# Fewer DMA transfers per sequence, constant rows loaded per home, late expert weights split on ScalarE and GpSimd, and new order lists for every engine

## The chip, the cores and the metric

The kernel runs on 1 core of a Trainium2 chip. The metric is device time in microseconds. Five engines work side by side, each through its own list of instructions in order: TensorE (PE, matrix products), VectorE (DVE), ScalarE (ACT), GpSimd (POOL), and SyncE (SP), which here issues every DMA transfer. They meet at semaphores only.

## The reference

One transformer layer on x of 16 sequences, 512 tokens, 128 features: layer norm, causal attention of 16 heads of size 64, a residual with a second layer norm (gamma, beta), layer norm again, and a mixture of 32 experts (top 8) with all experts computed for all tokens.

```python
q = jnp.einsum('bsd,hde->bhse', x, Wq); k = ...; v = ...
scores = jnp.where(causal, q k^T / sqrt(64), -inf); attn = softmax(scores)
y = x + heads @ Wo;  y = layernorm(y, eps=1e-3) * gamma + beta;  x = x0 + y
probs = softmax(h @ gate_w.T); top_w, top_idx = top_k(probs, 8); comb = normalised weights
for each expert: acc += (u * silu(g)) @ dw.T * w_e        # g, u = split(h @ guw.T)
```

## The kernel before

**Numbers.** Every float32 operand is used as a pair of float16 tiles, high and low, and a product is three matmuls (high*high, high*low, low*high). So for each product ScalarE writes the high half out of PSUM and VectorE the low half (`qk_high`/`qk_low`, `v_high`/`v_low`, `h_high`/`h_low`, `o_high`/`o_low`). For the softmax numerators ScalarE makes `p32` and `p_hi`, GpSimd `p_lo` (`p_low`, L1497).

**Order.** The order on each engine is written out by hand as a list of calls, `scores(n, 2, 1); values(n, 4, V); ...`. The second argument group names the PSUM bank (G, U, V, R0, R1; S0 and S1 belong to the scores, XB to the experts' sum). Sequences 0 and 1 are a prologue, a loop `for n in range(2, B - 2)` of 12 passes holds the steady state (each pass mixes the attention of sequence n with the experts of n - 2 and n - 1 and the projections of n + 1), and sequences 14 and 15 an epilogue, all with lists of their own.

**One head's scores.** Keys and queries of a pair of heads (`project`) are put by SP into one of five homes of `score_ops` (`place_qk`, L307 to L312, six transfers). Row maxima go around a longer way: `max_scores` (PE), `row_maximum` (DVE, L1124), `split_maxima` (POOL, L1486 to L1490), `turn_maxima` (PE), `copy_maxima` (ACT, L786), `place_max` (SP, L321, four transfers), and only then may `scores(m, 4g, 0)` start. Besides these, each home holds constant rows (the causal bars). Before the loop GpSimd copies them from the last home into the nine other halves (L1531, four copies of 64x4608 float16), on `rows_filled`.

**Experts.** `gate_product`, `gate_tanh`, `gate_times_tanh`, `up_product`, `times_up` (L1224) make a unit of two experts. The routing weights go to DRAM (`keep_weights`, L327, four transfers) and come back spread over 64 partitions for each of the two experts (`spread_weights`, L335, two transfers a unit). GpSimd multiplies (`weigh_unit`, L1512) and makes the low half (`unit_low`, L1516), PE does `down_product`. For the last sequence VectorE multiplies in float32 (`weigh_last`) and no halves are made.

**Weights.** They are loaded as float32 and split once, in 11 parts of `SPLIT`: w_hi by ScalarE (`halve`, L790), w_lo by VectorE (`rest`, L1067). Parts 0 and 1 (Wq, Wk) are on the way to the first projection, 2 and 3 are Wv and Wo, 4 to 10 the experts'. Their scales come from `largest`, `diagonal` (L1052) and `powers` on VectorE. A sequence has 103 transfers: 48 of `place_qk`, 16 of `place_max`, 4 of `keep_weights`, 32 of `spread_weights`, and 3 of x and y.

Of the kernel before, what the change touches and what calls it, by code (L numbers as in the profile page):

```python
# [11 lines left out]
P = 128  # L12
# [3 lines left out]
C = S // P  # L16
# [19 lines left out]
PARTS = 11  # L36
# [17 lines left out]
def layer(nc, x, wq, wk, wv, wo, gamma, beta, gate, gate_up, down, ident_c, mask_c,  # L54
          key_rows_c, query_rows_c, tail_c, out):
    with ExitStack() as ctx:
# [219 lines left out]
        def _(sp):  # L276
# [25 lines left out]
            def place_qk(m, q):  # L302
                slot = slot_of(m, q)
                if m == 0 and q == 2:
                    sp.wait_ge(w_lo_done, 3)
# [8 lines left out]
            def place_max(m, g):  # L314
                wait(sp, score_mm, UNITS * 2 * (m * PAIRS + 2 * g + 1 - SLOTS + 1))
                sp.wait_ge(rowmaxT_ready, m * QUADS + g + 1)
# [12 lines left out]
            def spread_weights(p, j):  # L329
                if j == 0:  # L330
                    sp.wait_ge(comb_stored, 16 * C * (p + 1))
# [14 lines left out]
            sp.wait_ge(w_lo_done, 2)  # L346
            place_qk(0, 0); load_xb(0); load_x(1); place_qk(0, 1); place_max(0, 0); place_qk(0, 2); place_qk(0, 3)
            place_qk(0, 4); place_max(0, 1); place_qk(0, 5); load_x(2); place_qk(0, 6); place_max(0, 2); place_qk(0, 7)
            place_max(0, 3); place_qk(1, 0); place_qk(1, 1); place_qk(1, 2); place_max(1, 0); place_qk(1, 3)
            place_qk(1, 4); place_max(1, 1); load_xb(1); place_qk(1, 5); place_max(1, 2); place_qk(1, 6)  # L350
            keep_weights(0); spread_weights(0, 0); spread_weights(0, 1); load_x(3); place_qk(1, 7); spread_weights(0, 2)
            spread_weights(0, 3); place_max(1, 3); spread_weights(0, 4); spread_weights(0, 5); spread_weights(0, 6)
            place_qk(2, 0); place_qk(2, 1); spread_weights(0, 7); spread_weights(0, 8); spread_weights(0, 9)
            place_max(2, 0); place_qk(2, 2); spread_weights(0, 10); place_qk(2, 3); spread_weights(0, 11)
            spread_weights(0, 12); spread_weights(0, 13); spread_weights(0, 14); place_qk(2, 4)

            for n in range(2, B - 2):
                place_max(n, 1); spread_weights(n - 2, 15); load_x(n + 2); place_qk(n, 5); place_max(n, 2)
                place_qk(n, 6); store(n - 2); place_qk(n, 7); keep_weights(n - 1); spread_weights(n - 1, 0)
                spread_weights(n - 1, 1); spread_weights(n - 1, 2); spread_weights(n - 1, 3); place_max(n, 3)  # L360
                spread_weights(n - 1, 4); place_qk(n + 1, 0); spread_weights(n - 1, 5); spread_weights(n - 1, 6)
                spread_weights(n - 1, 7); load_xb(n); place_qk(n + 1, 1); spread_weights(n - 1, 8)
                spread_weights(n - 1, 9); place_qk(n + 1, 2); place_max(n + 1, 0); spread_weights(n - 1, 10)
                spread_weights(n - 1, 11); place_qk(n + 1, 3); spread_weights(n - 1, 12); spread_weights(n - 1, 13)
                spread_weights(n - 1, 14); place_qk(n + 1, 4)

            place_max(14, 1); spread_weights(12, 15); place_qk(14, 5); place_qk(14, 6); place_max(14, 2); load_xb(14)
            store(12); place_qk(14, 7); keep_weights(13); spread_weights(13, 0); spread_weights(13, 1)
            spread_weights(13, 2); spread_weights(13, 3); spread_weights(13, 4); place_max(14, 3); spread_weights(13, 5)
            place_qk(15, 0); spread_weights(13, 6); spread_weights(13, 7); place_qk(15, 1); spread_weights(13, 8)  # L370
            place_max(15, 0); spread_weights(13, 9); spread_weights(13, 10); place_qk(15, 2); place_qk(15, 3)
            spread_weights(13, 11); spread_weights(13, 12); place_max(15, 1); place_qk(15, 4); spread_weights(13, 13)
            spread_weights(13, 14); spread_weights(13, 15); place_qk(15, 5); place_max(15, 2); place_qk(15, 6)
            load_xb(15); place_qk(15, 7); store(13); keep_weights(14); spread_weights(14, 0); spread_weights(14, 1)
# [3 lines left out]
            spread_weights(14, 14); spread_weights(14, 15); store(14); load_down(15); keep_weights(15)  # L378
# [8 lines left out]
        def _(pe):  # L387
# [73 lines left out]
            def scores(m, h, u):  # L461
# [1170 lines left out]
```

## Time and profile before

| | |
|---|---|
| median of 3 runs | 1748.65 us (1747.98 to 2051.43) |
| the profiled execution, its own time | 1747.59 us |
| its span, first to last instruction | 1745.7 us |
| mean granted TensorE clock | 0.991 |
| PE busy | 1633.9 us, 94% |
| DVE, ACT, POOL busy | 1462.4, 1404.4, 1403.9 us (84%, 80%, 80%) |

The page of the profile gives busy time by engine. Its list of waits says which engine stood idle for whom. The windows view splits the span into stretches, and the timeline lists instructions in order of time with the idle time before each in square brackets. PE's waits appear twice, for the matmul (PE) and for its weight load (PEld).

### The profile page before, as it was taken

What the parts mean: (1) busy time and instruction counts of PE and PEld (TensorE: products, weight loads), DVE (VectorE), ACT (ScalarE), POOL (GpSimd) and SP (SyncE); (2) the same over time, 40 slices, a digit from 0 to 9 for tenths busy, and PEclk for the clock granted to TensorE, in tenths of its full rate; (3) what the DMA queues carried; (4) which work ended last, traced back from release to release, by engine and by line L of the source; (5) the groups of instructions that cost most, each with busy time, mean ns of one, the idle gap of its engine ahead of it and who ended that gap; (6) DMA issues with size and microseconds to landing.
All of it is one profiled execution on the core that took longest, in us unless ns stands there. A gap on an engine that the chain in (4) does not pass through costs nothing.

```text
span 1745.7 us, 56980 instructions
## 1 busy us (share of the span) xinstructions
PE 1633.9 (94%) x21209; PEld 1113.7 (64%) x21209; DVE 1462.4 (84%) x4484; ACT 1404.4 (80%) x2364; POOL 1403.9 (80%) x1164
## 2 busy tenths in 40 slices
PE   3799999999999999999999999999999999999868
PEld 1366766666666666666666666666676666667655
DVE  7999889797887978879797887979889797887757
ACT  2799888797887879788797888879788787888752
POOL 4477997888879788887888979788897888889880
PEclk9999999999999999999999999999999999999999
DMA  5554554646455464544646454473645546435423
GB/s 181 128 122 106 145 136 123 166 106 158 104 132 129 106 178 110 142 115 115 174 106 159 110 140 124 104 186 95 158 117 133 139 106 165 123 109 138 112 79 105
DMA packets 219444, 226.26 MB, mean 130 GB/s; under 512 B 27041, under 2 KB 185249, under 8 KB 218913
## 3 DMA queue, kind: packets, MB, share of 16 engines
q1 hardware_dynamic: 219168, 222.61, 49.8%
q8 instruction: 170, 2.79, 0.7%
q14 instruction: 106, 0.86, 0.2%
HBM read 82.53 MB, written 5.24 MB: 50 GB/s over the span
## 4 chain that ended last, share of the span: by engine, by line
PE 61%; SPq 8%; DVE 8%; DMA 6%; POOL 6%; issue 5%; ACT 5%; POOLq 0%; ACTq 0%; DVEq 0%
PE bank_r L389 15%; PE bank_s L389 12%; PE bank_v L389 8%; PE bank_g L389 8%; PE bank_u L389 8%; PE bank_x L389 7%; SPq L321 3%; POOL p_lo L1497 2%; DMA expert_room<-comb_rows 2%; SPq L335 2%; SPq L311 1%; SPq L312 1%; POOL expert_room L1512 1%; DMA xt<-in_x 1%; SPq L310 1%
## 5 line engine op out<-in xcount | busy, mean ns | idle before, releaser
L1497 POOL TENSOR_TENSOR p_lo<-p,p_hi 128x1280 f16<-128x1280 f32 x256 | 674.7, 2636 | 149.0 <-ACT p_hi L786 148.2
L848 ACT ACTIVATE p<-bank_s,back 128x512 f32<-128x512 f32 (+1 forms) x768 | 461.4, 615 | 61.9 <-PE bank_s L389 53.8
L389 PE MATMUL bank_s<-score_ops 128*128 128x62 f16 (+10 forms) x4096 | 405.6, 233 | 20.6 <-DMA score_ops<-rowmaxT 15.3
L389 PEld LDWEIGHTS bank_s<-score_ops 128*128 128x128 f16 x4096 | 278.1, 97 | 192.5 <-issue 46.8
L1512 POOL TENSOR_TENSOR expert_room<-expert_room 128x512 f32<-128x512 f32 x240 | 304.4, 1275 | 34.7 <-DMA expert_room<-comb_rows 17.4
L786 ACT ACTIVATE p_hi<-p 128x1280 f16<-128x1280 f32 x256 | 324.6, 1268 | 7.8 <-PE bank_r L389 2.2
L1516 POOL TENSOR_TENSOR halves<-expert_room,halves 128x512 f16<-128x512 f32 x240 | 276.4, 1162 | 29.0 <-ACT halves L786 27.3
L1124 DVE CUSTOM_DVE_ANT_0 max_junk<-bank_r,mask 128x384 f16<-128x384 f32 (+3 forms) x523 | 232.1, 474 | 36.6 <-PE bank_g L389 16.3
L389 PE MATMUL bank_x<-w_hi,halves 128*128 128x128 f16 x1920 | 199.1, 220 | 2.0 <-POOL halves L1516 2.0
L786 ACT ACTIVATE halves<-expert_room 128x512 f16<-128x512 f32 x240 | 150.1, 625 | 44.8 <-POOL expert_room L1512 32.2
L389 PE MATMUL bank_x<-w_lo,halves 128*128 128x128 f16 x960 | 173.2, 220 | 0.0
L389 PEld LDWEIGHTS bank_x<-w_hi,halves 128*128 128x128 f16 x1920 | 155.2, 98 | 20.3 <-issue 6.2
L389 PE MATMUL bank_r<-nat 64*128 64x384 f16 (+3 forms) x523 | 106.1, 300 | 15.3 <-DVE o L1137 9.8
L1124 DVE CUSTOM_DVE_ANT_0 max_junk<-bank_u,mask 128x512 f16<-128x512 f32 (+3 forms) x202 | 99.0, 505 | 6.1 <-PE bank_g L389 4.0
L389 PE MATMUL bank_r<-tanh_room,w_hi 128*128 128x512 f16 x338 | 101.8, 383 | 0.5 <-DVE o L1137 0.4
L389 PEld LDWEIGHTS bank_x<-w_lo,halves 128*128 128x128 f16 x960 | 94.1, 98 | 7.3
L389 PE MATMUL bank_r<-v_hi,p_hi 128*128 128x65 f16 x870 | 87.9, 194 | 2.1 <-POOL p_lo L1497 1.4
L389 PE MATMUL bank_r<-v_hi,p_lo 128*128 128x65 f16 x870 | 87.9, 194 | 0.0
L389 PE MATMUL bank_r<-v_lo,p_hi 128*128 128x64 f16 x870 | 87.8, 192 | 0.0
L786 ACT ACTIVATE nat<-bank_r 128x512 f16<-128x512 f32 x110 | 65.9, 599 | 26.2 <-PE bank_r L389 24.1
L389 PE MATMUL bank_u<-tanh_room,w_hi 128*128 128x512 f16 x264 | 78.7, 380 | 7.5 <-DVE v_lo L1112 6.2
L1124 DVE DVE_READ_ACCUMULATOR2_ANT rowmax<- 128x1 f32 x1024 | 85.2, 83 | 0.1
(298 smaller groups left out, 5015.4 us busy)
## 6 DMA issues: line engine op xcount, KB each, us to landing
score_ops<-nat SPq DMA_DIRECT2D x256, 256.0 KB, 3.8
score_ops<-nat SPq DMA_DIRECT2D x512, 128.0 KB, 3.6
expert_room<-comb_rows SPq DMA_DIRECT2D x480, 128.0 KB, 3.0
xt<-in_x SPq DMA_DIRECT2D x16, 256.0 KB, 3.5
xb<-in_x SPq DMA_DIRECT2D x16, 256.0 KB, 4.1
score_ops<-rowmaxT SPq DMA_DIRECT2D x256, 2.0 KB
out_y<-expert_room SPq DMA_DIRECT2D x16, 256.0 KB, 3.4
score_ops<-comb_rows SPq DMA_DIRECT2D x32, 128.0 KB, 3.0
```

Source lines behind the costliest of these rows:

```text
L310: sp.dma_start(score_ops[0:E, 0:4, slot, ab, :], home[rows, K_HI:K_HI + 1].to_broadcast([E, 4, S])).then_inc(placed[q], 16)
L311: sp.dma_start(score_ops[0:E, 4:6, slot, ab, :], home[rows, Q_HI:Q_LO + 1]).then_inc(placed[q], 16)
L312: sp.dma_start(score_ops[E:P, 0:5:4, slot, ab, :], home[rows, K_LO:Q_HI + 1]).then_inc(placed[q], 16)
L321: sp.dma_start(home[part:part + 1], rowmaxT[at:at + 8, :]).then_inc(max_placed[g], 16)
L335: sp.dma_start(weighed(p, j)[ED * e:ED * e + ED, :], comb_rows[2 * j + e:2 * j + e + 1, :].to_broadcast([ED, S])).then_inc(spread_sem(p, j ...
L389: return pe.matmul(dst, lhsT, rhs, start=start, stop=stop, skip_group_check=shared)
L786: return act.activation(dst, src, ACT.Copy)
L848: act.activation(p32[:, h % P_SLOTS, at:at + cols], bank[score_bank(h, u)][:, 0:cols], ACT.Exp, scale=back[:, SC_SCORE:SC_SCORE + 1]).then ...
L1124: done = dve.tensor_tensor_reduce(max_junk[:, k % 2, at:at + cols], bank[b][:, at:at + cols], mask[:, S - cols:S], 1.0, NEG, ALU.add, ALU. ...
L1497: pool.tensor_tensor(p_lo[:, slot, :], p32[:, slot, :], p_hi[:, slot, :], ALU.subtract).then_inc(p_lo_done, 1)
L1512: pool.tensor_tensor(weighed(p, j), weighed(p, j), unit(p, j), ALU.mult).then_inc(a32_done, 1)
L1516: pool.tensor_tensor(a_lo[:, j % 2, :], weighed(p, j), a_hi[:, j % 2, :], ALU.subtract).then_inc(a_lo_done, 1)
```

## The change

1. Transfers. `place_max` issues 2 and not 4 (both rows at once), `keep_weights` 1 and not 4, `spread_weights` 1 and not 2 for a unit (128 partitions). A sequence has 76 and not 103. What waits for them counts 32, 16 and 16 instead of 64, 64 and 32.
2. Constant rows. The one load into the last home and GpSimd's four copies are gone. `fill_rows(slot)` loads both halves of a home from DRAM by two transfers (384 KB and 128 KB), ten in all, put between the first placings. `place_max` of sequence 0 waits on SP for them.
3. Late weights. Parts 4 to 10: ScalarE makes w_hi as before and then scales the source in place, GpSimd subtracts (`rest_late`). VectorE keeps parts 0 to 3.
4. `weigh_last` moves from VectorE to GpSimd.
5. All five lists are written anew. Nothing is computed differently, and each list holds the same calls apart from those named above.

```diff
+            def fill_rows(slot):
+                sp.dma_start(score_ops[E:P, 1:4, slot], key_rows_c).then_inc(rows_filled[slot], 16)
+                sp.dma_start(QB[E:P, slot], query_rows_c).then_inc(rows_filled[slot], 16)
...
-                    for part in range(2):
-                        at = 16 * k + 8 * part
-                        sp.dma_start(home[part:part + 1], rowmaxT[at:at + 8, :]).then_inc(max_placed[g], 16)
+                    sp.dma_start(home, rowmaxT[16 * k:16 * k + 16, :]).then_inc(max_placed[g], 16)
...
-                for c in range(C):
-                    sp.dma_start(comb_rows[:, c * P:c * P + P], combT[c * NE:c * NE + NE, :]).then_inc(comb_stored, 16)
+                sp.dma_start(comb_rows.rearrange("e (c p) -> c e p", c=C), combT).then_inc(comb_stored, 16)
...
-                for e in range(2):
-                    sp.dma_start(weighed(p, j)[ED * e:ED * e + ED, :],
-                                 comb_rows[2 * j + e:2 * j + e + 1, :].to_broadcast([ED, S])).then_inc(spread_sem(p, j), 16)
+                both = comb_rows[2 * j:2 * j + 2].rearrange("a (b s) -> a b s", b=1)
+                sp.dma_start(weighed(p, j), both.to_broadcast([2, ED, S])).then_inc(spread_sem(p, j), 16)
...
+                if part >= EARLY:
+                    w = SPLIT[part][0]
+                    act.activation(source(part), source(part), ACT.Copy, scale=w_scale[:, w:w + 1]).then_inc(late_scaled, 1)
...
+            def rest_late(part):
+                w, at, cols = SPLIT[part]
+                pool.wait_ge(w_hi_done, part + 1)
+                pool.wait_ge(late_scaled, part - EARLY + 1)
+                pool.tensor_tensor(wl(w, at, cols), source(part), wh(w, at, cols), ALU.subtract).then_inc(late_lo_done, 1)
...
-            pool.wait_ge(ln_shift[0], 1)
-            pool.wait_ge(rows_loaded, 80)
-            for side in (KB0, KB1, KB2, QB):
-                rows = side[E:P].rearrange("p a b s -> p (a b) s")
-                pool.tensor_copy(rows[:, 0:2 * SLOTS - 1, :], rows[:, 2 * SLOTS - 1:2 * SLOTS, :].to_broadcast([E, 2 * SLOTS - 1, S])).then_inc(rows_filled, 1)
...
-                spread_weights(n - 1, 9); place_qk(n + 1, 2); place_max(n + 1, 0); spread_weights(n - 1, 10)
+                place_max(n + 1, 0); spread_weights(n - 1, 10); place_qk(n + 1, 2); spread_weights(n - 1, 11)
```

**SP, in the loop, around `place_max(n + 1, 0)`.** Rows of before: the spreading of two units, `place_qk(n + 1, 2)`, then the four transfers of `place_max`, then two more units.

```order
L335 DMA expert_room<-comb_rows 64x512 x4
L310 DMA score_ops<-nat 64x4x512
L311 DMA score_ops<-nat 64x2x512
L312 DMA score_ops<-nat 64x2x512
L310 DMA score_ops<-nat 64x4x512
L311 DMA score_ops<-nat 64x2x512
L312 DMA score_ops<-nat 64x2x512
L321 DMA score_ops<-rowmaxT 1x8x128 x4
L335 DMA expert_room<-comb_rows 64x512 x4
```

The same place of the change:

```order
L339 DMA expert_room<-comb_rows 128x1x512 x3
L326 DMA score_ops<-rowmaxT 2x8x128 x2
L339 DMA expert_room<-comb_rows 128x1x512
L314 DMA score_ops<-nat 64x4x512
L315 DMA score_ops<-nat 64x2x512
L316 DMA score_ops<-nat 64x2x512
```

`place_max(n + 1, 0)` now stands ahead of `place_qk(n + 1, 2)` and is two transfers long.

**GpSimd, in the prologue, behind the first norm.** Rows of before, from the last instruction of `inverse_deviation` to `keep_h(0)`:

```order
L1472 TENSOR_TENSOR shift<-minus_mean,rstd 128x4
L1531 COPY score_ops<-score_ops 64x4608 x4
L1486 TENSOR_SCALAR rowmax<-rowmax 128x16
L1488 CAST turnable<-rowmax 128x2x8
L1490 TENSOR_TENSOR turnable<-rowmax,turnable 128x2x8
L1480 COPY h_cur<-h 128x512
```

The same place of the change:

```order
L1472 TENSOR_TENSOR shift<-minus_mean,rstd 128x4
L1486 TENSOR_SCALAR rowmax<-rowmax 128x16
L1488 CAST turnable<-rowmax 128x2x8
L1490 TENSOR_TENSOR turnable<-rowmax,turnable 128x2x8
L1496 TENSOR_TENSOR w_lo<-expert_room,w_hi 128x1024 x2
L1480 COPY h_cur<-h 128x512
```

The four copies are gone from the head of the list, and the first two of seven `rest_late` (L1496) stand behind `split_maxima(0, 0)`; the others follow one by one among the `p_low` of sequence 0.

## Rows read from the trace of the kernel before

**Rows 1.** Windows view, from the span's start; first row names the columns.
```profile
core 0: us, PE busy (x) PEld busy (x) DVE busy (x) ACT busy (x) POOL busy (x), PEclk, DMA share, GB/s
24.00:58.00 34.00, 20.92 (x75) 6.46 (x76) 31.66 (x70) 11.29 (x19) 8.35 (x6) 0.95 0.33 78
58.00:131.00 73.00, 65.02 (x928) 44.28 (x927) 67.81 (x232) 66.56 (x107) 47.88 (x32) 0.98 0.59 136
...
234.50:1485.50 1251.00, 1209.31 (x15950) 829.79 (x15949) 1062.55 (x3324) 1051.86 (x1777) 1064.18 (x889) 1.00 0.52 132
1485.50:1692.00 206.50, 194.79 (x2592) 134.55 (x2590) 156.27 (x463) 162.95 (x272) 179.80 (x145) 0.99 0.42 111
1692.00:1745.70 53.70, 39.37 (x247) 25.64 (x243) 37.65 (x80) 15.22 (x27) 2.74 (x6) 0.87 0.35 110
```

**Rows 2.** Waits in 234:1486, PE then PEld: total us, times, longest.
```profile
PE bank_s L389 <- DMA score_ops<-rowmaxT: 14.9, 12, 2.2
PE bank_r L389 <- DVE o L1137: 9.8, 12, 0.9
PE bank_u L389 <- DVE v_lo L1112: 6.2, 5, 1.4
PE bank_x L535 <- DVE comb L1210: 4.4, 12, 0.4
...
PEld bank_r L389 <- DVE hT L1102: 10.9, 12, 1.0
```

**Rows 3.** Timeline of the prologue: start, duration, engine, instruction, idle before.
```profile
13.24 17.93 POOL L1531 COPY score_ops<-score_ops 64x4608 f16<-64x4608 f16 x4 [6.26 <-DMA tail<-in_tail]
13.40 9.90 DVE L1067 SCALAR_TENSOR_TENSOR w_lo<-score_ops,w_scale,w_hi 128x1024 f16<-128x1024 f32 x2 [1.22 <-ACT w_hi L790]
...
23.96 1.03 PE L389 MATMUL bank_r<-hT,w_hi 128*128 128x512 f16 x2 [11.93 <-DVE hT L1102]
...
27.27 3.92 DVE L1052 TENSOR_SCALAR w_diagonal<-ident,w_peak 2x2 f32<-2x2 f32 x1
```

**Rows 4.** Single lines of the kernel: duration in ns, min/median/max.
```profile
L1067 DVE SCALAR_TENSOR_TENSOR w_lo<-expert_room,w_scale,w_hi x4: 1254/1278/2015, 76.4 to 98.4; 128x1024 f16<-128x1024 f32 x4
...
L1052 DVE TENSOR_SCALAR w_diagonal<-ident,w_peak x3: 218/219/3921, 10.1 to 56.4; 11x11 f32<-11x11 f32 x1, 2x2 f32<-2x2 f32 x1, 7x7 f32<-7x7 f32 x1
...
L790 ACT ACTIVATE w_hi<-expert_room,w_scale x4: 1132/1139/1148, 59.2 to 81.3; 128x1024 f16<-128x1024 f32 x4
...
L1497 POOL TENSOR_TENSOR p_lo<-p,p_hi x256: 2607/2623/3653, 68.5 to 1675.8; 128x1280 f16<-128x1280 f32 x128
```

**Rows 5.** Timeline 520 to 534: ACT, SP and PE around `place_max(n + 1, 0)`.
```profile
525.73 0.27 ACT L786 ACTIVATE rowmaxT<-bank_v 32x128 f16<-32x128 f32 x1 [1.39 <-PE bank_v L389]
...
524.12 0.74 SPq L310 DMA_DIRECT2D score_ops<-nat  x1
...
528.96 2.80 SPq L321 DMA_DIRECT2D score_ops<-rowmaxT  x4
...
532.93 0.38 PE L389 MATMUL bank_s<-score_ops 128*128 128x512 f16 x1 [0.75 <-DMA score_ops<-rowmaxT]
```

**Rows 6.** Timeline 76 to 99, a low half on VectorE beside GpSimd.
```profile
77.18 6.48 POOL L1497 TENSOR_TENSOR p_lo<-p,p_hi 128x1280 f16<-128x1280 f32 x2 [2.14 <-ACT p_hi L786]
79.16 2.02 DVE L1067 SCALAR_TENSOR_TENSOR w_lo<-expert_room,w_scale,w_hi 128x1024 f16<-128x1024 f32 x1
```

**Rows 7.** DMA issues: count, KB each, median us to landing (page, part 6).
```profile
expert_room<-comb_rows SPq DMA_DIRECT2D x480, 128.0 KB, 3.0
```

**Rows 8.** The last stage: timeline, chain of waits, and GpSimd's weighing (ns).
```profile
1715.90 20.45 SPq L335 DMA_DIRECT2D score_ops<-comb_rows  x32
...
1738.58 3.58 PE bank_x L389 x32
...
L1512 POOL TENSOR_TENSOR expert_room<-expert_room x16: 1263/1279/1310, 1018.4 to 1089.5; 128x512 f32<-128x512 f32 x16
```

More of the change, by code:

```diff
@@ L315, in place_max @@
                 wait(sp, score_mm, UNITS * 2 * (m * PAIRS + 2 * g + 1 - SLOTS + 1))
+                if m == 0:
+                    for slot in range(2 * g, min(2 * g + 2, SLOTS)):
+                        sp.wait_ge(rows_filled[slot], 32)
                 sp.wait_ge(rowmaxT_ready, m * QUADS + g + 1)
@@ L351, in _ @@
[L351 to L355, printed above, removed]
@@ new lines, in _ @@
+            scores(1, 2, 1); max_scores(1, 4, 0, G, U); project(1, 10, R1); times_wo(0, 3, V); scores(1, 2, 2)
+            values(1, 5, G); turn_maxima(1, 1, U); scores(1, 3, 0); scores(1, 3, 1); max_scores(1, 4, 1, R0, V)
+            times_v(1, 0, U); scores(1, 3, 2); project(1, 11, R1); times_v(1, 1, V); max_scores(1, 4, 2, G, R0)
+            scores(1, 4, 0); max_scores(1, 5, 0, R1, U); project(1, 12, G); values(1, 6, R0); scores(1, 4, 1)
+            times_v(1, 2, V); scores(1, 4, 2); project(1, 13, U); scores(1, 5, 0); times_v(1, 3, R1)
@@ new lines, in _ @@
+            turn_heads(1, 0, G); scores(1, 5, 1); max_scores(1, 5, 1, V, R0); scores(1, 5, 2); values(1, 7, R1)
+            project(1, 14, U); turn_h2(0); max_scores(1, 5, 2, R0, G); turn_heads(1, 1, V); scores(1, 6, 0)
+            times_v(1, 4, R1); gate_product(0, 0, G); turn_maxima(1, 2, R0); logit_product(0); scores(1, 6, 1)
+            gate_product(0, 1, R1); scores(1, 6, 2); max_scores(1, 6, 0, U, G); times_wo(1, 0, V); scores(1, 7, 0)
+            turn_h(2, R0); project(1, 15, U); scores(1, 7, 1); times_v(1, 5, V); scores(1, 7, 2)
@@ new lines, in _ @@
+            max_scores(1, 7, 2, G, R1); up_product(0, 3, R0); scores(1, 10, 2); turn_heads(1, 3, U); times_v(1, 8, G)
+            scores(1, 11, 0); values(2, 0, R0); project(2, 2, R1); gate_product(0, 5, U); times_wo(1, 1, G)
+            times_v(1, 9, V); up_product(0, 4, R0); turn_maxima(1, 3, R1); down_product(0, 0); max_scores(2, 0, 0, G, U)
+            max_scores(2, 0, 1, R1, R0); project(2, 3, V); scores(1, 11, 1); scores(1, 11, 2); gate_product(0, 6, U)
+            values(2, 1, R1); max_scores(2, 0, 2, R0, G); scores(1, 12, 0); down_product(0, 1); up_product(0, 5, R0)
@@ new lines, in _ @@
+            up_product(0, 8, V); project(2, 5, G); scores(1, 15, 0); scores(1, 15, 1); down_product(0, 4)
+            max_scores(2, 2, 0, U, V); turn_maxima(2, 0, R0); times_wo(1, 2, R1); times_v(1, 13, U)
+            max_scores(2, 2, 1, V, G); scores(1, 15, 2); gate_product(0, 9, R1); down_product(0, 5)
+            gate_product(0, 10, U); turn_heads(1, 6, V); max_scores(2, 2, 2, R1, R0); scores(2, 0, 0); scores(2, 0, 1)
+            project(2, 6, R1); up_product(0, 9, G); down_product(0, 6); project(2, 7, R0); times_v(1, 14, V)
@@ new lines, in _ @@
+            scores(2, 0, 2); times_v(1, 15, R1); max_scores(2, 3, 0, V, G); project(2, 8, U); up_product(0, 10, R0)
+            project(2, 9, V); down_product(0, 7); turn_heads(1, 7, R1); down_product(0, 8); max_scores(2, 3, 1, U, G)
+            gate_product(0, 11, R0); scores(2, 1, 0); scores(2, 1, 1); times_wo(1, 3, R1); max_scores(2, 3, 2, U, R0)
+            scores(2, 1, 2); times_v(2, 0, G); down_product(0, 9); up_product(0, 11, U); scores(2, 2, 0)
+            gate_product(0, 12, V); turn_maxima(2, 1, R1); down_product(0, 10)
@@ new lines, in _ @@
+            max_scores(14, 7, 1, U, V); scores(14, 9, 2); times_wo(14, 0, R1); scores(14, 10, 0); project(15, 0, R0)
+            turn_weights(13); scores(14, 10, 1); scores(14, 10, 2); gate_product(13, 1, U); up_product(13, 0, V)
+            up_product(13, 1, G); times_v(14, 8, R0); times_v(14, 9, V); project(15, 1, R1); turn_heads(14, 3, U)
+            max_scores(14, 7, 2, R0, G); gate_product(13, 2, V); scores(14, 11, 0); up_product(13, 2, R1)
+            gate_product(13, 3, R0); values(15, 0, G); times_wo(14, 1, V); turn_heads(14, 4, R1)
```

1190 lines of the change are left out of this document (584 added, 606 removed).

## The prediction

> **What bounds the kernel.** I read the windows view first. In the steady loop [rows 1] PE is busy for 1209.31 of 1251.00 us, in 12 passes of 104.25 us each. VectorE, ScalarE and GpSimd are each busy for about 85% of it. So PE's own products set the loop, and at most 1251.00 − 1209.31 = 41.7 us are there to be taken. Outside the loop it differs. In the stretch 24 to 58 PE is busy for 20.92 of 34 us and VectorE for 31.66: VectorE sets the pace. In 58 to 131 three engines are all near 90% (65.02, 67.81, 66.56 of 73). The epilogue has 206.50 − 194.79 = 11.7 us idle.
>
> The waits of PE in the loop come next [rows 2]. The maxima's last transfer ends a wait of 14.9 us in 12 times (once a pass), hT of VectorE 10.9 us and o 9.8 us (12 each), v_lo 6.2 us in 5, comb 4.4 us in 12. The timeline of the prologue [rows 3] shows one large wait: PE's first projection starts at 23.96 after 11.93 us of waiting for hT, which VectorE could not make before its two `rest`.
>
> **The change, in the order of time.**
>
> *Constant rows.* GpSimd's four copies run from 13.24 for 17.93 us [rows 3]. Two `rest` of 128x1024 lie beside them and take 9.90 us, where the four late ones have a median of 1.278 [rows 4]. Without copies the two take 2 × 1.28 = 2.6, so 7.3 us go from the path to the first projection. One of the tiny `w_diagonal` beside the copies takes 3.92 and not 0.22 us [rows 3, 4], 3.7 us more, again on VectorE where it is the bound. Together 11.0.
>
> A rule of the Trainium skill bears on this (SBUF — State Buffer, section "Who interferes with whom"): a VectorE instruction with two SBUF inputs contends with a GpSimd instruction that reads SBUF, and whichever starts first holds the shared ports throughout. The 9.90 us fit it in kind. It also speaks against item 3 below, where I come back to it.
>
> What replaces the copies is ten transfers on SP. An issue on SP costs 0.64 to 0.74 us [rows 5, 8], so 6.4 to 7.4 us of SP time, spread between the first placings, when SP's next hard need is the placing of maxima for the first scores. I take 0; the cover is SP's free time before the first placing, and if that is gone it costs the whole 7.4.
>
> *Late weights.* VectorE loses seven `rest`: four of 1024 columns (4 × 1.28 = 5.1) and three smaller ones, some 8 us in all. GpSimd gets seven `rest_late`. Their price isn't in the trace; the nearest row is `p_low`, also a subtraction of an fp16 half, with 2.62 us for 1280 columns [rows 4], so 2.62 × 1024/1280 = 2.1 each, under 15 us, less than the 17.93 it loses. ScalarE gets six or seven in-place scalings at 1.14 [rows 4], some 7 us, and in 58 to 131 it has 73 − 66.6 = 6.4 us free [rows 1]. So VectorE's relief is about eaten up by ScalarE. I take −1; bounds +7 (all of it on ScalarE as bound) and −8 (all of VectorE's relief).
>
> Beside it, from rows: one `rest` beside a `p_low` took 2.02 us in place of 1.28 [rows 6], so a `rest_late` that runs beside VectorE's `rest(3)` costs 0.7 us. By the Trainium skill's rule in that same section the loser stands for the whole of the other's instruction, which by the estimate above would be 2.1 us. That would make the sum 35 or 34 where it is 36 below. The row, a third of an instruction rather than all of it, is the nearer guide, and neither changes the forecast.
>
> Prologue: −11 − 1 = **−12**, bounds −19 and −4 (fills not hidden).
>
> *The loop.* Take the first scores of a pass [rows 5]. `copy_maxima` ends at 525.73 + 0.27 = 526.0. SP is then still in the six placings of `place_qk(n + 1, 2)` that it began at 524.12, and starts the four transfers of the maxima only at 528.96, ending 2.80 us later (0.70 each). PE starts the scores at 532.93, after 0.75 us of waiting. Now SP has `place_max` ahead of `place_qk`, and two transfers: 526.0 + 1.4 = 527.4 for the last issue, in place of 531.76. That is 4.4 us earlier, with a longest wait of 2.2 [rows 2]. So all 14.9 go.
>
> hT's 10.9: two more `qk_high` now stand ahead of `h_high` on ScalarE, but more of PE's work (`scores`, `times_wo`) stands between the turn of h and the next use of bank R1. I take half, 5. v_lo's 6.2: the same, 3. comb's 4.4: the wait is at most 0.4 each, and several PE groups (`values`, two `up_product`) now stand in between; all 4.4. o's 9.8: same neighbours, so 0. Gain 14.9 + 5 + 3 + 4.4 = 27.4.
>
> Against it: at two places, groups 0 and 2, `turn_maxima` now follows the last `max_scores` after less PE work, so VectorE's `row_maximum` and GpSimd's `split_maxima` have less time. Where GpSimd is in a `p_low` just then, 2.62 us are added [rows 4]. No row shows a wait there now. The bounds are 0 and 2 × 2.62 = 5.2 us a pass (63 us in 12); I take 0.5 a pass, 6 us: less PE work stands between than before, but some still does. Loop: **−21**, bounds −40 (all idle time) and, below, the slower rival.
>
> Fewer issues by themselves (27 a sequence) relieve SP only; they count where SP is waited for, which is in the 14.9.
>
> *The end.* `weigh_last` on GpSimd: 16 × 1.279 = 20.5 us [rows 8]. The first spreading is issued at 1715.90 and lands 3.0 us later [rows 7, 8]: GpSimd starts about 1719.5 and ends about 1740.0. Three transfers fewer for `keep_weights` (3 × 0.64 = 1.9) bring this to 1738.1, beside PE's last products at 1738.58 to 1742.16 [rows 8]. So it is just hidden: 0, or up to +2 if `keep_weights` isn't what is waited for. With the spreading halved from 32 to 16 issues, SP (20.45 us before) is no longer what paces it. The epilogue's new order: I take −3 of its 11.7 idle [rows 1], as the same placings wait there; bounds 0 and −8.
>
> **Sum.** −12 − 21 − 3 = −36. The profiled execution's own time is 1747.59, so 1711.6. The median of before lies 1.1 above it, so I forecast **1712 us**. The line at 2%, about what a measurement of this kernel can tell from no change, is 1748.65 × 0.98 = 1713.7. The forecast stands almost on it.
>
> **The rivals.**
>
> *A, nearly all waits go.* For it: PE's idle in the loop is 41.7 us, and each wait is short (0.4 to 2.2 each), so a better order can hide them. Taking 19 in the prologue, 31 in the loop and 8 at the end gives 1748.65 − 58 = 1691. Against it: ends of waits are handed on to the next engine.
>
> *B, the loop's gain is handed on.* VectorE and GpSimd at 85% of the loop have dense parts; a wait removed in front of them comes back behind. Then the loop keeps 2 us, with the prologue's 12 and 3: about 1732. For it: hT, o, v_lo and comb are all VectorE's. Against it: the largest, 14.9, is SP's own order.
>
> *C, slower.* GpSimd holds `split_maxima` behind a `p_low` at both places in each pass. Then 5.2 us a pass in place of 0.5: 1712 + (63 − 6) = 1769. It decides the sign once the new wait is above 0.5 + 36/12 = 3.5 us a pass. Against it: GpSimd idles 15% of the loop, and PE's cover absorbs part.
>
> *D, the change doesn't do what it says in the loop and the prologue waits for SP's fills.* Prologue −4, the rest 0 to −3: about 1743.
>
> **Chances.** Forecast (1700 to 1724) 0.50; A 0.18; B 0.20; C 0.07; D 0.05. The range has to leave out no more than 2 in 10: C, D and the better half of A go out, so 1692 to 1741. Faster by over 2% (below 1713.7): half of the forecast's 0.50 and a little more (0.30), and A: 0.48. Within 2%: the other 0.20, B, D, and those of C's weaker forms: 0.49. Slower by over 2%: 0.03. The forecast case's own range is 1700 to 1724.
>
> **What would show it.** In the profile after: the two early `rest` together near 2.6 us, PE's first projection at about 16.7, no `w_diagonal` above 0.3 us, and first scores some 9 to 11 us earlier. In 58 to 131 ScalarE is not above 97%. In the loop a pass takes about 102.5 us, PE's wait for the maxima's transfer is gone, and the new waits (`turn_maxima` for GpSimd's halves) add up to less than 10 us. At the end PE works without a break through the last units. The forecast is wrong if the first projection still waits for something else (the loads of x or of the weights), if the wait for maxima comes back as one for GpSimd or VectorE, or if PE waits for GpSimd in the last stage.

## The result, and the profile after

The changed kernel takes 2502.96 us (median of 4 runs, 2502.35 to 2505.06), where the kernel before takes 1750.16 beside it. The ratio is 1.431, with a 95% interval of 1.428 to 1.434. So it is 43% slower, where I forecast 1712 us and gave slower 3 in 100. One of the four runs of the kernel before was a slow one (2051.43 us); the ratios here compare fast runs only. No rival came near it: the slowest, C, was 1769.

The profiled execution has a span of 2500.6 us against 1745.7. Windows of the changed kernel, in the columns of [rows 1]: the two prologue stretches, then from PE's first to its last instruction of the loop, and a piece of the last stage.

```profile
24.00:58.00 34.00, 22.82 (x108) 8.40 (x109) 30.57 (x95) 20.02 (x31) 10.49 (x12) 0.85 0.82 173
58.00:131.00 73.00, 69.09 (x1030) 48.23 (x1029) 61.99 (x227) 70.96 (x119) 56.58 (x43) 1.00 0.61 142
253.90:2075.60 1821.70, 1340.22 (x15951) 887.52 (x15949) 1059.77 (x3312) 1045.38 (x1777) 1066.78 (x889) 0.86 0.34 90
2430.00:2470.00 40.00, 25.63 (x94) 15.57 (x94) 6.72 (x10) 2.75 (x4) 10.11 (x8) 0.62 0.13 50
```

To 131 us all is well: PE is busy for 69.09 us of 73 where it was 65.02. Behind it a pass of the loop takes 1821.7 / 12 = 151.8 us and not 104.25. The loss of 754.9 us splits into 19.4 up to the loop, 570.7 in it, and 164.8 behind it. VectorE, ScalarE and GpSimd do the same work in the same time as before (1059.77 against 1062.55, and so on). PE idles for 1821.70 − 1340.22 = 481.5 us where it idled for 41.7. It is also busy for 131 us longer with the same products, since the granted clock fell from 1.00 to 0.86.

PE's waits in the loop (254 to 2075), then GpSimd's, in the columns of [rows 2]:

```profile
PE bank_s L392 <- DMA score_ops<-rowmaxT: 251.4, 36, 17.9
PE bank_x L392 <- POOL halves L1527: 133.2, 24, 9.6
PE bank_g L392 <- DVE expert_room L1226: 43.4, 12, 4.0
```
```profile
POOL expert_room L1518 <- DMA expert_room<-comb_rows: 371.0, 98, 6.9
POOL p_lo L1503 <- ACT p_hi L790: 265.7, 96, 12.1
```

GpSimd's largest wait is 371.0 us for the spread weights to land, where it was 17.4 over the whole of the kernel before. The last stage shows the reason barest, because there nothing else is transferred. Timeline of GpSimd and PE in it (start, duration, engine, instruction, idle before):

```profile
2431.02 1.26 POOL L1523 TENSOR_TENSOR score_ops<-score_ops 128x512 f32<-128x512 f32 x1 [3.94 <-DMA score_ops<-comb_rows]
2432.43 2.05 PE L392 MATMUL bank_x<-p,score_ops 128*128 128x128 f32 x8 [4.07 <-POOL score_ops L1523]
...
2436.24 1.26 POOL L1523 TENSOR_TENSOR score_ops<-score_ops 128x512 f32<-128x512 f32 x1 [3.95 <-DMA score_ops<-comb_rows]
```

GpSimd gets a unit every 5.2 us. All that time the DMA share is 0.13, which is 2 of 16 engines (0.125); before, with 128 partitions in two transfers, it was 0.60 between 1716 and 1736. So the transfer of a unit, 128 rows of 2 KB, ran on two engines: 64 rows each, worked out as 5.2 / 64 = 0.08 us a row.

SP feels it too. Issues of `spread_weights` (L339) by the view of that line (ns, min/median/max), and SP's own timeline in a pass of the loop (`...` marks rows left out, here and below):

```profile
L339 SPq DMA_DIRECT2D expert_room<-comb_rows x240: 474/547/5792, 160.5 to 2367.2; - x120
L339 SPq DMA_DIRECT2D score_ops<-comb_rows x16: 503/5094/7213, 2407.7 to 2474.3; - x16
```
```profile
505.00 5.27 SPq L314 DMA_DIRECT2D score_ops<-nat  x1
...
516.11 14.01 SPq L339 DMA_DIRECT2D expert_room<-comb_rows  x3
534.00 1.37 SPq L326 DMA_DIRECT2D score_ops<-rowmaxT  x2
```

One placing of keys (L314) takes 5.27 us to issue behind such transfers; in the kernel before one took 0.74 [rows 5]. The three spreadings from 516.11 stretch over 14 us, issue and waits for a free buffer together, and the placing of the maxima stands behind them at 534.00.

### The profile page after: what moved, and what is told of

The parts are those of the page before. It is cut to its first block, busy times and chain, and to the rows that moved or that the text cites. A ratio compares the mean times of both kernels' runs of the same rounds, so it can differ in the third digit from the quotient of the medians.

```text
span 2500.6 us, 56565 instructions
## 1 busy us (share of the span) xinstructions
PE 1817.5 (73%) x21209; PEld 1197.1 (48%) x21209; DVE 1434.2 (57%) x4461; ACT 1404.0 (56%) x2371; POOL 1417.7 (57%) x1183
## 4 chain that ended last, share of the span: by engine, by line
PE 34%; DMA 33%; SPq 14%; ACT 7%; issue 7%; POOL 5%; DVE 1%; POOLq 0%; ACTq 0%; DVEq 0%
DMA expert_room<-comb_rows 22%; PE bank_r L392 9%; DMA score_ops<-rowmaxT 8%; PE bank_s L392 8%; PE bank_v L392 5%; SPq L339 5%; PE bank_x L392 5%; PE bank_u L392 4%; PE bank_g L392 2%; SPq L326 2%; SPq L298 2%; SPq L315 2%; POOL p_lo L1503 2%; ACT p L855 1%; DMA comb_rows<-expert_room 1%
## 5 line engine op out<-in xcount | busy, mean ns | idle before, releaser
L1131 DVE CUSTOM_DVE_ANT_0 max_junk<-bank_r,mask 128x512 f16<-128x512 f32 (+3 forms) x475 | 218.6, 489 | 17.6 <-PE bank_r L392 9.5
L1131 DVE CUSTOM_DVE_ANT_0 max_junk<-bank_u,mask 128x128 f16<-128x128 f32 (+3 forms) x193 | 85.2, 460 | 237.8 <-PE bank_r L392 232.8
L1226 DVE SCALAR_TENSOR_TENSOR expert_room<-tanh_room,bank_g 128x512 f32<-128x512 f32 x134 | 91.3, 682 | 153.2 <-POOL expert_room L1518 82.2
L392 PE MATMUL bank_g<-tanh_room,w_hi 128*128 128x512 f16 x324 | 113.7, 437 | 43.4 <-DVE expert_room L1226 43.4
L790 ACT ACTIVATE nat<-bank_r 128x512 f16<-128x512 f32 x152 | 89.7, 600 | 72.8 <-PE bank_r L392 49.0
L1114 DVE TENSOR_TENSOR nat<-bank_r,nat 128x512 f16<-128x512 f32 x152 | 102.9, 684 | 48.2 <-ACT nat L790 46.7
L392 PE MATMUL bank_r<-nat 64*128 64x512 f16 (+3 forms) x475 | 98.0, 314 | 35.4 <-DVE expert_room L1226 27.7
L892 ACT ACTIVATE tanh_room<-bank_g,back 128x512 f32<-128x512 f32 x137 | 94.2, 687 | 46.4 <-PE bank_g L392 44.6
L392 PE MATMUL bank_v<-v_hi,p_hi 128*128 128x65 f16 x1020 | 105.5, 196 | 9.1 <-POOL p_lo L1503 9.1
L392 PEld LDWEIGHTS bank_v<-v_hi,p_hi 128*128 128x128 f16 x1020 | 94.1, 99 | 23.5 <-issue 12.4
## 6 DMA issues: line engine op xcount, KB each, us to landing
expert_room<-in_gate_up SPq DMA_DIRECT2D x1, 2048.0 KB, 10.4
```

Source lines behind the costliest of these rows:

```text
L392: return pe.matmul(dst, lhsT, rhs, start=start, stop=stop, skip_group_check=shared)
L790: return act.activation(dst, src, ACT.Copy)
L892: act.activation(th, bank[b][:, :], ACT.Tanh, scale=back[:, SC_HALF:SC_HALF + 1]).then_inc(th_done, 1)
L1114: dve.tensor_tensor(nat[:, q % 2, (K_LO, Q_LO)[w], :], bank[b][:, :], nat[:, q % 2, (K_HI, Q_HI)[w], :], ALU.subtract).then_inc(proj_lo, 1)
L1131: done = dve.tensor_tensor_reduce(max_junk[:, k % 2, at:at + cols], bank[b][:, at:at + cols], mask[:, S - cols:S], 1.0, NEG, ALU.add, ALU. ...
L1226: dve.scalar_tensor_tensor(unit(p, j), th, 1.0, bank[b][:, :], ALU.add, ALU.mult).then_inc(gth_done, 1)
```

## The experiments

Theory T: the merged transfer of a unit runs on two of 16 DMA engines, and this alone carries the loss; the rest of the change is worth about what the prediction said. Rival U: the new lists or GpSimd's late weights carry it. Rival V: one transfer of 128 partitions with a repeated source is slow by its size or form. Rival W, for the runs that store the weights several times: not the number of engines counts but the store of copies. The kernels go by the labels (e1 to e12) that the expectations use. A time of one run has no interval; for the others the ratio to the kernel before, run beside them, is given.

**e1. The changed kernel with two transfers a unit** (GpSimd's waits for them count 32 again).

```diff
-                both = comb_rows[2 * j:2 * j + 2].rearrange("a (b s) -> a b s", b=1)
-                sp.dma_start(weighed(p, j), both.to_broadcast([2, ED, S])).then_inc(spread_sem(p, j), 16)
+                for e in range(2):
+                    sp.dma_start(weighed(p, j)[ED * e:ED * e + ED, :],
+                                 comb_rows[2 * j + e:2 * j + e + 1, :].to_broadcast([ED, S])).then_inc(spread_sem(p, j), 16)
```

> The changed kernel, with only spread_weights put back into two transfers a unit (64 partitions each). Theory T (the one transfer of a unit runs on two of the 16 DMA engines, 5.1 us each, 82 us a sequence on the same two engines, and SP and GpSimd wait for it): the loss goes with it, the time comes to 1700 to 1745 us, DMA share in the last stage back near 0.6 from 0.13. If the prediction's other terms hold, 1712. Rival U (the new lists or the late weights on GpSimd carry the loss): above 2000 us.

Measured: 1704.88 us, ratio 0.9746 (0.9724 to 0.9768). One edit of one transfer takes all of the loss away and leaves a kernel 2.5% faster than before. Its windows:

```profile
58.00:131.00 73.00, 69.08 (x1027) 48.01 (x1027) 62.14 (x226) 71.09 (x119) 56.77 (x43) 1.00 0.62 143
...
224.80:1444.70 1219.90, 1197.58 (x15953) 822.30 (x15951) 1060.25 (x3312) 1035.65 (x1777) 1062.10 (x889) 1.00 0.52 134
```

U falls: lists, late weights, fills and the other merged transfers are all still in it.

**e2. The kernel before with one transfer a unit.** The reverse of that edit, in the kernel before.

> The kernel before, with only spread_weights put into one transfer a unit as in the change. Theory T: most of the loss appears by this edit alone, 2300 to 2650 us, DMA share 0.13 in the last stage. Rival U: 1750 to 1800 us.

Measured: 2510.56 us (one run), with a DMA share of 0.13 between 2450 and 2480. The edit alone, in the old lists, makes the whole loss. U is out from both sides.

**e3, e4, e5. How many engines.** The transfer stays one for a unit, but each row of weights is stored 8, 2 or 4 times, so that the source's outermost count is 16, 4 or 8 and not 2. For 8 copies:

```diff
-                sp.dma_start(comb_rows.rearrange("e (c p) -> c e p", c=C), combT).then_inc(comb_stored, 16)
+                for c in range(C):
+                    one = combT[c * NE:c * NE + NE, :].rearrange("e (k p) -> e k p", k=1)
+                    sp.dma_start(comb_rows[:, :, c * P:c * P + P], one.to_broadcast([NE, 8, P])).then_inc(comb_stored, 16)
...
-                both = comb_rows[2 * j:2 * j + 2].rearrange("a (b s) -> a b s", b=1)
-                sp.dma_start(weighed(p, j), both.to_broadcast([2, ED, S])).then_inc(spread_sem(p, j), 16)
+                both = comb_rows[2 * j:2 * j + 2].rearrange("e k (b s) -> (e k) b s", b=1)
+                sp.dma_start(weighed(p, j), both.to_broadcast([16, ED // 8, S])).then_inc(spread_sem(p, j), 16)
```

> The changed kernel, with one transfer a unit kept (256 KB, 128 partitions, 16 issues a sequence), but its source has 16 outermost rows and not 2: keep_weights stores each row of weights 8 times (four transfers, 512 KB written a sequence and not 64). Theory T, in the form that the outermost count of the source sets on how many DMA engines a transfer runs: as fast as with two transfers, 1700 to 1745 us. Rival V (one transfer of 128 partitions with a repeated source is slow by its size or by its form): stays above 2300 us.

> As e3, but each row is stored twice, so the source's outermost count is 4. Theory T: four engines, a unit takes 5.1 / 2 = 2.6 us on each of them, 41 us a sequence; DMA share in the last stage 0.25; with the 44 us of other transfers per pass this is below a pass of 104 us, so the time falls most of the way, to 1720 to 1850 us. Rival V: above 2300 us.

> As e3 and e4, each row of weights stored 4 times, so the source's outermost count is 8. Theory T: eight engines, 1.3 us a unit on each, 20 us a sequence. With two, four and sixteen at 2503, 2056 and 1741 us, the time lies between the last two and nearer the last, 1745 to 1850 us; SP's issues over 1.2 us nearly gone. Rival W (it is not the number of engines but the store of copies that changes with it): outside that, above 1950 or below 1735.

Measured: 8 copies 1741.40 us, ratio 0.9953 (0.9936 to 0.9969); 4 copies 1842.26; 2 copies 2056.20 (one run each). Windows in the last stage while the spread weights are on their way, for 2, 4 and 8 copies:

```profile
2010.00:2035.00 25.00, 20.57 (x114) 14.24 (x115) 6.71 (x10) 4.12 (x6) 11.84 (x10) 0.86 0.26 101
```
```profile
1812.00:1822.00 10.00, 8.20 (x57) 6.54 (x58) 3.62 (x6) 2.55 (x4) 9.23 (x8) 1.00 0.53 199
```
```profile
1707.50:1722.00 14.50, 12.33 (x70) 8.82 (x70) 7.00 (x11) 4.12 (x7) 11.00 (x9) 0.88 0.95 234
```

The DMA share is 0.26, 0.53, 0.95: 4, 8 and 15 or 16 of 16 engines, and 0.13 in the changed kernel. The spreading has the same bytes, destination and number of transfers each time. V falls, and T holds in its exact form: the source's outermost count sets the engines. That it is the count and not the number of different rows in DRAM, the transfers of before say: each reads one row 64 times and lands 3.0 us after its issue [rows 7], where one engine at 0.08 us a row would take 5. With two copies GpSimd gets a unit every 2.6 us, half of 5.2:

```profile
2016.28 1.27 POOL L1525 TENSOR_TENSOR score_ops<-score_ops 128x512 f32<-128x512 f32 x1 [1.35 <-DMA score_ops<-comb_rows]
2018.89 1.26 POOL L1525 TENSOR_TENSOR score_ops<-score_ops 128x512 f32<-128x512 f32 x1 [1.34 <-DMA score_ops<-comb_rows]
```

My expectation for two copies (1720 to 1850) missed. I had asked whether the engines have enough time in a pass (85 us of 104) and not what the longer way of each unit does. Passes took 104.3 us with 16 engines, 111.5 with 8, 125.0 with 4. Per unit the engines' time is, worked out from 5.2 on two, 0.65, 1.3 and 2.6 us. So 7.2 us more a pass than with 8 copies stand for 16 × 0.65 = 10.4 more, and 20.7 for 16 × 1.95 = 31. In the changed kernel it is 151.8 − 101.7 = 50.1 over e1, for 16 × 4.55 = 73. Each time the pass pays about 0.7 of what all units' transfers grew by, long before any engine is full.

Rival W fell with e5: more copies are stored from e4 to e5 to e3, and the time falls. But 8 copies stay 36 us above e1, 31.6 of them in the loop, and there the store is the likely cause. It takes four issues and not one, and from the first of them to the first spreading 5.4 us pass with 8 copies, 5.6 with 4 (1802.36 to 1807.95) and 2.5 in e1 (1668.88 to 1671.38). With 8 copies PE waits at one place in each pass for a unit of VectorE, a wait that comes to 1.1 us in all in e1. That the late store stands behind it is argued, not tried:

```profile
PE bank_g L394 <- DVE expert_room L1228: 27.1, 12, 3.2
```

**e12. Is the long wait a matter of order?** In the changed kernel PE's wait at `scores(n, 4, 0)` is 15.5 to 17.9 us a pass, 16.8 on average. One move on SP, otherwise the changed kernel (the first and the last pass take it over from, and hand it to, the lists around the loop):

```diff
-                load_x(n + 2); place_max(n, 1); spread_weights(n - 2, 15); place_qk(n, 5); place_qk(n, 6)
+                load_x(n + 2); place_max(n, 1); spread_weights(n - 2, 14); spread_weights(n - 2, 15); place_qk(n, 5); place_qk(n, 6)
...
-                spread_weights(n - 1, 14)
```

> The changed kernel as it is (one transfer a unit, on two engines), with the single move of e11: spread_weights(n-1,14) behind place_max(n,1). In the changed kernel scores(n,4,0) waits 17.0 us a pass for that place_max, the largest of PE's waits (204 us in 12 passes). If the wait is only SP's order, it goes: 2290 to 2350 us. If it stands for the slow chain of the units themselves (each unit's extra 4.5 us lies in the loop SP, transfer, GpSimd, free buffer, SP), it is handed on to the down products and the next placings: 2420 to 2510.

Measured: 2436.34 us (one run), 66 us less.

```profile
PE bank_s L391 <- DMA score_ops<-rowmaxT: 195.1, 36, 12.5
PE bank_x L391 <- POOL halves L1526: 135.8, 24, 9.5
```

The wait for maxima fell from 251.4 to 195.1 and that for GpSimd's halves stayed. The time lies in the range of my second case, but not for its reason: next to nothing is handed on. The loop gains 60.9 us (1821.7 to 1760.8), about what the wait at `scores(n, 4, 0)` loses in 12 passes (202 to 140), and the rest of that wait, 10.5 to 12.5 us a pass, stands at the same place. There the maxima's own transfer is late. The same pass in the changed kernel and in this one:

```profile
876.75 2.96 SPq L326 DMA_DIRECT2D score_ops<-rowmaxT  x2
886.65 0.58 PE L392 MATMUL bank_s<-score_ops 128*128 128x512 f16 x1 [16.46 <-DMA score_ops<-rowmaxT]
```
```profile
849.74 2.60 SPq L326 DMA_DIRECT2D score_ops<-rowmaxT  x2
857.84 0.59 PE L391 MATMUL bank_s<-score_ops 128*128 128x512 f16 x1 [11.50 <-DMA score_ops<-rowmaxT]
```

From the end of the issue to PE's start 6.9 and 5.5 us pass, for 4 KB in each transfer; in the kernel before it was 1.2 (531.76 to 532.93, [rows 5]). So the move takes away what SP's order cost, and what is left is the slow way of what is already issued. That the units' slow way is a circle of SP's issue, transfer, GpSimd and free buffer fits these rows, but no run took the circle itself apart (with more than four buffers, say).

**e6. Fills alone, in the kernel before.** GpSimd's four copies out, ten transfers of `fill_rows` in, with the waits that they need.

```diff
-            place_qk(0, 0); load_xb(0); load_x(1); place_qk(0, 1); place_max(0, 0); place_qk(0, 2); place_qk(0, 3)
-            place_qk(0, 4); place_max(0, 1); place_qk(0, 5); load_x(2); place_qk(0, 6); place_max(0, 2); place_qk(0, 7)
+            place_qk(0, 0); load_x(1); fill_rows(0); fill_rows(1); place_qk(0, 1); load_xb(0); fill_rows(2)
+            place_max(0, 0); place_qk(0, 2); fill_rows(3); place_qk(0, 3)
+            place_qk(0, 4); place_max(0, 1); place_qk(0, 5); fill_rows(4); load_x(2);
+            place_qk(0, 6); place_max(0, 2); place_qk(0, 7)
```

> The kernel before, with only the constant rows changed: fill_rows for the five homes in SP's prologue in place of GpSimd's four copies. By the prediction's term: 11 us less (7.3 of the two early low halves, 3.7 of w_diagonal), 1735 to 1742 us, the two early low halves near 2.6 us. Rival (the fills delay placings as much as the copies delayed VectorE): 1746 to 1752.

Measured: 1741.59 us, ratio 0.9930 (0.9908 to 0.9951), which is 12 us less (9 to 16). Its timeline, against [rows 3]:

```profile
13.44 2.48 DVE L1073 SCALAR_TENSOR_TENSOR w_lo<-score_ops,w_scale,w_hi 128x1024 f16<-128x1024 f32 x2 [1.22 <-ACT w_hi L796]
...
16.58 1.03 PE L394 MATMUL bank_r<-hT,w_hi 128*128 128x512 f16 x2 [4.51 <-DVE hT L1108]
...
19.88 0.22 DVE L1058 TENSOR_SCALAR w_diagonal<-ident,w_peak 2x2 f32<-2x2 f32 x1
...
223.96 0.62 PE L394 MATMUL bank_s<-score_ops 128*128 128x384 f16 x8
```

2.48 for 9.90, 0.22 for 3.92, and the first projection at 16.58 for 23.96. The last row is PE's first product of the loop, which came at 234.5 before: 10.5 us earlier.

**e7. Maxima in four transfers.** e1 with `place_max` of before.

```diff
-                    sp.dma_start(home, rowmaxT[16 * k:16 * k + 16, :]).then_inc(max_placed[g], 16)
+                    for part in range(2):
+                        at = 16 * k + 8 * part
+                        sp.dma_start(home[part:part + 1], rowmaxT[at:at + 8, :]).then_inc(max_placed[g], 16)
```

> e1 with place_max back at four transfers, all in the new order. If the count of transfers matters by itself, each place_max ends 1.4 us later and the scores that wait for it (0.9 us a pass in e1 at the second group) wait longer: 5 to 17 us more than e1, 1710 to 1722. If only the order matters: 1703 to 1708.

Measured: 1730.16 us, ratio 0.9867 (0.9840 to 0.9895), 0.0121 above e1: 21 us, more than the 5 to 17 I expected. The count of transfers counts by itself: the loop takes 17.3 us longer and begins 5.0 later. Waits of PE in the loop, e1 and then this one:

```profile
PE bank_s L393 <- DMA score_ops<-rowmaxT: 8.3, 8, 1.6
```
```profile
PE bank_s L395 <- DMA score_ops<-rowmaxT: 22.1, 16, 3.0
```

**e8. Order alone, in the kernel before.**

```diff
-                spread_weights(n - 1, 9); place_qk(n + 1, 2); place_max(n + 1, 0); spread_weights(n - 1, 10)
+                spread_weights(n - 1, 9); place_max(n + 1, 0); place_qk(n + 1, 2); spread_weights(n - 1, 10)
```

> The kernel before, in the loop of SP place_max(n+1,0) moved ahead of place_qk(n+1,2), nothing else. The prediction took all 14.9 us of the wait for the maxima away by this move and two transfers fewer. By it 1733 to 1740 us. Rival (the wait is handed on to the keys and queries placed later, or to the next engine): 1743 to 1750.

Measured: 1729.09 us, ratio 0.9864 (0.9849 to 0.9879): 24 us less. Two calls swapped on SP give more than the 14.9 us of the wait, and a time below the 1733 to 1740 us I expected. PE's wait for the maxima's transfer in the loop, 14.9 in [rows 2], is

```profile
PE bank_s L389 <- DMA score_ops<-rowmaxT: 0.7, 2, 0.4
```

and the loop's 12 passes take 1231.4 us and not 1251.0. PE's idle time there fell by 15.4 us, the wait and little more, and its busy time by 4.2. Nothing was handed on.

**e9. `weigh_last` back on VectorE,** in e1, put between its last gate and up products.

```diff
-            times_up(15, 8, G); gate_times_tanh(15, 9, U); gate_times_tanh(15, 10, R1); gate_times_tanh(15, 11, R0)
+            times_up(15, 8, G); weigh_last(15, 0); weigh_last(15, 1); gate_times_tanh(15, 9, U); weigh_last(15, 2)
+            gate_times_tanh(15, 10, R1); weigh_last(15, 3); weigh_last(15, 4); gate_times_tanh(15, 11, R0)
...
-            second_inverse(15); weigh_last(15, 0); weigh_last(15, 1); weigh_last(15, 2); weigh_last(15, 3)
+            second_inverse(15)
```

> e1 with weigh_last of the last sequence back on VectorE, put between its last gate and up products as before the change. The prediction costed the move at 0: 1702 to 1708 us. If GpSimd's 20.5 us chain now ends last, this is 2 to 5 us faster than e1; if VectorE's last stretch is freed by the move, it is 2 to 5 us slower.

Measured: 1709.21 us, ratio 0.9770 (0.9748 to 0.9792), 4 us above e1 with intervals that overlap. The windows from the last routing weights to the last product lean the same way, e1 and then this one:

```profile
1668.60:1699.60 31.00, 30.98 (x205) 22.53 (x204) 18.56 (x29) 9.08 (x14) 20.03 (x16) 1.00 0.46 139
```
```profile
1671.90:1708.60 36.70, 32.95 (x206) 23.96 (x204) 27.84 (x44) 9.11 (x14) 0.00 (x0) 0.95 0.38 117
```

But the profiled execution here is the slowest of its four (1714.13 us, the others 1707.25 to 1709.30), so its 5.7 us are too many. A gain by the move is not shown.

**e10. Late weights back on VectorE,** in e1: seven `rest`, without ScalarE's in-place scaling and without `rest_late`.

```diff
-                if part >= EARLY:
-                    w = SPLIT[part][0]
-                    act.activation(source(part), source(part), ACT.Copy, scale=w_scale[:, w:w + 1]).then_inc(late_scaled, 1)
...
-            row_maximum(0, 3, 2, 1, R1); row_maximum(0, 4, 0, 0, G); denominators(0, 0, R1); divide(0, 0, R1)
+            row_maximum(0, 3, 2, 1, R1); row_maximum(0, 4, 0, 0, G); denominators(0, 0, R1); rest(4); divide(0, 0, R1)
```

> e1 with the seven late low halves back on VectorE (about 1.28 us for 1024 columns), ScalarE's seven in-place scalings and GpSimd's seven subtractions gone. The prediction gave the move 1 us, bounds 7 slower and 8 faster. So 1704 to 1708 expected, up to 1713 if VectorE's relief counted in full, down to 1698 if ScalarE was the bound there.

Measured: 1714.02 us, ratio 0.9797 (0.9777 to 0.9818), 0.0051 above e1: 9 us, just beyond my upper bound. It lies in the prologue (the loop begins at 233.5 and not 224.8). PE in 58 to 131, where e1 has 69.08, and two instructions of its timeline:

```profile
58.00:131.00 73.00, 60.92 (x890) 42.54 (x889) 63.29 (x204) 60.23 (x99) 43.65 (x31) 0.98 0.55 126
```
```profile
87.97 2.61 POOL L1495 TENSOR_TENSOR p_lo<-p,p_hi 128x1280 f16<-128x1280 f32 x1 [1.05 <-ACT p_hi L791]
88.30 3.37 DVE L1072 SCALAR_TENSOR_TENSOR w_lo<-expert_room,w_scale,w_hi 128x1024 f16<-128x1024 f32 x1
```

These 9 us are not the worth of the late weights. In e6 VectorE makes all late low halves too, in the old lists, and its loop begins at 223.96, 0.8 us before that of e1. So e10 prices `rest` put into lists that were written without it, at the places where I put it. Against the old order, late weights and the new order of the prologue together gain nothing.

**e11. A better version.** e1 with the move of e12 on SP.

> e1 with one move on SP: spread_weights(n-1,14), which waits for GpSimd to free a buffer, goes from ahead of place_max(n,1) to behind it (into the next pass). In e1 SP starts that place_max about 5 us after its maxima are ready and scores(n,4,0) waits 0.87 us a pass. If that wait goes: 6 to 10 us less than e1, 1695 to 1699. If the later spreading makes GpSimd and the down products wait as long: 1703 to 1710.

Measured: 1695.58 us, ratio 0.9689 (0.9673 to 0.9705). That is 3.1% faster than the kernel before, and 10 us less than e1. Here the same move pays in full: the loop takes 1210.7 us and not 1219.9, for a wait of 8.3, and PE's first waits in it are now

```profile
PE bank_r L392 <- DVE hT L1109: 4.7, 12, 0.4
PE bank_x L401 <- ACT y L809: 4.6, 12, 0.4
```

and none for a transfer.

## Why the prediction was wrong, and where it was right

**The step that failed** is in the terms "The loop" and "The end". Under the loop the prediction said of the merged transfers that fewer issues "relieve SP only". At the end it took the landing time of the transfer before (3.0 us, [rows 7], 64 partitions) for the new one, and said "With the spreading halved from 32 to 16 issues, SP (20.45 us before) is no longer what paces it". The merged transfer was thus priced as half the issues and an unchanged landing. No row of before showed a merged transfer, and the prediction gave it neither a bound nor a rival. What the runs showed in its place is 5.2 us of transfer a unit on two engines, one unit after the other, and 754.9 us in all: 19.4 up to the loop, 570.7 in it and 164.8 behind it. Edited alone it takes the loss away (e1) or makes it (e2). The place in the diff that held it is `to_broadcast([2, ED, S])`: outermost count 2.

The Trainium skill would have told. It says (DMA: Bandwidth & Descriptors, section "Why a DMA increments its semaphore by 16 and not by 1") that such a transfer runs on the largest number of engines, up to 16, which divides the outermost counts of both sides, counts of 1 left out. By that rule 2, 4, 8 and 16 engines come out for the change, e4, e5 and e3; this case's DMA shares 0.13, 0.26, 0.53 and 0.95 agree. The prediction weighed another page of the Trainium skill and did not hold each new transfer's shape against this one.

**Rivals.** All four were about waits that shift by a few us. C, the slow side, was to come from GpSimd's `split_maxima` behind a `p_low`. In e1 no such wait is among PE's larger ones; my price for it, 6 us, was too much. The loop's 31.1 us in e1 is what rival A gave it (31).

**The other terms, in kernels where they stand alone or the bad transfer is mended:**

| term | predicted | measured |
|---|---|---|
| constant rows | −11 | −12 (−9 to −16), e6; up to the loop −10.5 |
| late weights, with the prologue's new order | −1 (−8 to +7) | +0.8, e1 against e6 |
| `weigh_last` | 0 | −4, intervals overlap, e9 |
| prologue in all | −12 | −9.7, e1 |
| loop | −21 | −31.1, e1 |
| end | −3 | −1.5, e1 |
| sum, profiled | 1711.6 | 1705.2, e1 |

- *Constant rows:* mechanism and sizes as said (2.48 for the forecast 2.6, first projection 16.58 for 16.7). The ten fills on SP cost nothing that shows.
- *Late weights:* I let ScalarE, 66.56 of 73 us busy, eat VectorE's relief, and took −1. Next to nothing is what e1 and e6 show. Whether ScalarE is the reason (71.09 of 73 us busy in e1, over the 97% that I had set as a sign) no run took apart. `rest_late` took 2.13 to 2.15 us for the estimated 2.1. Of the six full late `rest` that e10 puts back three took 3.37, 2.52 and 1.57 us and not 1.28.
- *The port:* in e10 `p_low` starts at 87.97 and ends at 90.58. The `rest` that starts at 88.30 ends at 91.67. It took 2.1 us longer than the undisturbed 1.28, of the 2.3 us that this `p_low` still ran. I had taken "a third of an instruction" from [rows 6] as the nearer guide, and misread it. The first `p_low` of the pair there ends at about 77.18 + 2.62 = 79.8, the `rest` starts only at 79.16 and ends at 81.18, 1.4 us later: there was only 0.6 us of the `p_low` left to stand for. The rule of the Trainium skill that the prediction quotes (the loser stands for the whole of the other's instruction) fits both rows, read so that it stands until that instruction ends.
- *The loop:* the wait for the maxima went as said, and was worth more than its 14.9 us (e8: 24, of them 19.6 in the loop). PE's waits for o (9.8) and v_lo (6.2) are gone too where I left 9.8 and 3.1; hT stands at 4.7. Of the new lists I had credited too little. The count of maxima transfers, folded into "all 14.9 go", is worth 21 us by itself in the new order (e7), of them 17.3 in the loop. These two don't add up (17.3 + 19.6 is more than the loop's 31.1), and I take it (argued, not tried) that they partly remove the same lateness of SP.
- *Slips in the sums:* 14.9 + 5 + 3 + 4.4 is 27.3 and not 27.4, and 1711.6 + 1.1 is 1712.7, so 1713 and not 1712. What the range leaves out adds to 0.21, a little over its 2 in 10. None of this touches the outcome.

## What to carry to other kernels

Before transfers are merged, write down for each the outermost counts of both sides: a leading 2 (a repeated row, a pair) can leave a transfer with 2 of 16 engines, and the number of issues says nothing of that. An operation of the steady loop that has no row in the trace of before is the first to be bounded, whatever it saves; here a bound would have been its bytes over as many engines as its outermost count, two. Look at the share of busy DMA engines in a stretch where only one kind of transfer runs: 0.13 names the fault at a glance. And where SP's queue is long, ask what stands ahead of the transfer that PE waits for: swapping two calls gave 24 us (e8), and a move at another place 10 us on top of e1 (e11).

## What the runs showed of the hardware

- A transfer of 128 rows of 2 KB takes 5.2 us on 2 engines and 2.6 on 4 (the distance from unit to unit in the last stage), about 0.08 us a row and engine.
- Behind such transfers the issue of others grows too: up to 5.8 us for a `spread_weights` in the loop and 5.5 for a placing of 256 KB (L314, median 0.66; its longest in e1 is 1.6). So does the landing: the load of x (L298, 256 KB) lands 13.1 us after its issue (median), 3.7 in e1, and the maxima's 4 KB take 6.9 us in the row shown under e12.
- The granted clock was lower where PE idled more: 1.00 over the loop before (PE busy for 97% of it), 0.86 in the changed kernel (74%), 0.62 between 2430 and 2470 where PE is busy in short bursts (half of 2.4 GHz is 1.2, so this stretch is mostly at the lower level). Of the loop's 570.7 us, 131 are PE's own products made slower.
